# Out-degrees as rows of sums: a count matrix streamed past a column of ones in a two-layer graph network

## The reference

```python
h = maximum(layernorm(x), 0)
# layer 0: row = src, col = dst
h0 = h @ W_in + b_in                                   # 3125 x 64
deg = segment_sum(ones(50000), row, 3125)              # how many edges start at each node
dis = where(deg > 0, rsqrt(maximum(deg, 1)), 0)
cur = acc = h0
for _ in range(3):
    cur = segment_sum(cur[col] * (dis[row] * dis[col])[:, None], row, 3125)
    acc = acc + cur
x = x + (acc / 4) @ W_out + b_out
# layer 1: relational, 64 edge types built of 16 bases
h = maximum(layernorm(x), 0)
x = x + relu(segment_sum(msg(h[src], type, weight), dst, 3125) + h_bias + h @ loop_weight)
```

## Time and profile before

| | us |
|---|---|
| median of 3 runs | 986.79 (985.37 to 989.05) |
| profiled execution: time | 984.78 |
| profiled execution: span of the trace | 983.2 |
| PE busy / PEld busy | 785.8 / 584.1 |
| DVE busy | 719.5 |
| ACT busy / POOL busy | 355.4 / 471.9 |
| the 625 one-column products, first to last start | 239.8 to 297.3 |

### The profile page before, as it was taken

One profiled execution on the slowest core, in us unless ns is written; L12 is line 12 of the kernel. 1 busy time (PEld: TensorE's weight loads), 2 busy tenths in 40 slices (PEclk: granted clock), 3 DMA queues, 4 the chain that ended last, 5 costly groups with the idle time before them and its releaser, 6 DMA issues.

```text
span 983.2 us, 27231 instructions
## 1 busy us (share of the span) xinstructions
PE 785.8 (80%) x5974; PEld 584.1 (59%) x5975; DVE 719.5 (73%) x2379; ACT 355.4 (36%) x705; POOL 471.9 (48%) x568
## 2 busy tenths in 40 slices
PE   5666666667879999999179899898888888787876
PEld 3234333333558999998057677676666666555555
DVE  7999999998625644435167777777777877887885
ACT  0422577898760000013154444433433332222100
POOL 2186433231000000101377777777777777777773
PEclk8798999999658999999579999999999999999999
DMA  4022457896330000112951221221211111211213
GB/s 123 22 67 67 117 138 141 159 170 144 98 94 6 2 2 1 34 41 87 293 139 51 54 53 51 53 54 51 53 53 52 53 52 52 54 51 53 54 51 93
DMA packets 64853, 73.32 MB, mean 75 GB/s; under 512 B 12804, under 2 KB 53179, under 8 KB 64667
## 3 DMA queue, kind: packets, MB, share of 16 engines
q1 hardware_dynamic: 48362, 37.30, 15.3%
q0 software_dynamic: 16432, 35.29, 14.3%
HBM read 43.85 MB, written 8.22 MB: 53 GB/s over the span
## 4 chain that ended last, share of the span: by engine, by line
PE 34%; DVE 26%; issue 15%; DVEq 10%; POOL 8%; DMA 5%; ACT 2%; SPq 1%; POOLq 0%; ACTq 0%
PE ps L1211 16%; PE ps L1288 10%; POOL CT L677 7%; DVE ohbuf L843 7%; DVE CT L985 5%; DVE u L843 4%; DMA CT<-h_dram,src_col 4%; PE ps L1119 4%; DVE CT L988 3%; DVEq L988 3%; DVEq L127 3%; PE ps L1267 2%; DVEq L985 2%; DVE ohbuf L838 2%; DVEq L843 1%
## 5 line engine op out<-in xcount | busy, mean ns | idle before, releaser
L677 POOL DMA_INDIRECT CT<-h_dram,src_col x391 | 370.5, 948 | 126.7 <-issue 105.4
L1288 PE MATMUL ps<-CT 128*128 128x256 f32 x1180 | 302.6, 405 | 65.4 <-DVE CT L985 31.7
L1288 PEld LDWEIGHTS ps<-CT 128*128 128x128 f32 x1180 | 203.0, 191 | 159.2 <-issue 142.1
L988 DVE SCALAR_TENSOR_TENSOR CT<-ps,dlP,CT 128x256 f32<-128x256 f32 x580 | 279.4, 482 | 4.5
L985 DVE COPY CT<-CT 128x128 f32 x590 | 148.3, 251 | 123.6 <-PE ps L1288 54.7
L1430 ACT COPY CT<-ps 128x256 f32<-128x256 f32 x200 | 77.6, 388 | 307.1 <-PE ps L1288 303.6
L1119 PE MATMUL ps<-ohbuf 128*128 128x400 bf16 x395 | 103.5, 368 | 42.3 <-DVE ohbuf L843 18.6
L1368 ACT CAST stage<-ps 128x800 bf16<-128x800 f32 x100 | 82.3, 823 | 75.6 <-PE ps L1119 74.5
L1211 PE MATMUL ps<-u,CT 128*128 128x192 bf16 x1250 | 105.0, 246 | 0.9 <-DVEq L951 0.9
L1211 PEld LDWEIGHTS ps<-u,CT 128*128 128x128 bf16 x1250 | 103.1, 98 | 1.9 <-DVEq L951 1.1
L843 DVE TENSOR_SCALAR ohbuf<-iota,keys 128x400 bf16<-128x400 int16 x395 | 103.1, 324 | 0.0
(11 more groups left out here) (186 smaller groups left out, 619.5 us busy)
## 6 DMA issues: line engine op xcount, KB each, us to landing
CT<-stage SPq DMA_DIRECT2D x200, 100.0 KB, 3.5
u<-types_dram POOLq DMA_DIRECT2D x49, 128.0 KB, 3.6
CT<-h_dram,src_col POOLq DMA_INDIRECT x391, 2.5
coef_dram<-coef_out POOLq DMA_DIRECT2D x49, 64.0 KB, 3.8
CT<-coef_dram SPq DMA_DIRECT2D x1, 3048.0 KB, 11.0
out<-CT SPq DMA_DIRECT2D x4, 256.0 KB
ohbuf<-x SPq DMA_DIRECT2D x3, 320.0 KB, 3.8
x_dram<-ohbuf SPq DMA_DIRECT2D x3, 320.0 KB, 2.7
```

The lines of the kernel that those rows point to most:

```text
L677: pool.indirect_dma_start(out=gring[:, (j + 1) % GRING, :], out_offset=None, in_=h2_dram, in_offset=bass.IndirectOffsetOnAxis(ap=src_col[: ...
L988: dve.scalar_tensor_tensor(kpair[:, u, :, :], nodes.unsqueeze(1).broadcast_to([P, BASES, WIN]), dl, coef_flat[:, ds(tiles * -BASES + NT * ...
L1288: pe.matmul(ps[:, ds(summed.place(counts[u][0], RING), 1), 0:WIN * BASES], gpair[:, u, :], kpair[:, u, :, :].rearrange("p b d -> p (b d)") ...
```

## The change

The degree sums are turned round. The stationary operand becomes a matrix of seven columns, all zero but one column of ones (a slice of `pick_row`, chosen so that the ones stand at column `i`), and `CT[:, k, :]` is streamed past it, 512 columns at a time: seven products for a group `k` (six of 512 columns and one of 128) instead of 25. Row `i` of bank 7 collects the sums of sources 512 i to 512 i + 511. At the end ACT copies the 7 x 512 sums to SBUF (`deg_rows`, in the space of `keys`), and four float32 products with an identity turn them to columns in the bank `COEF_BANK`, in another order of columns, which DVE's two comparisons read in two pieces each. POOL makes `pick_row` at the start (two memsets and a wait), so that the count on which DVE and PE wait at the start, `PC0`, is 14 instead of 12. The twelve products of zeros stand behind the turning and go to bank 7.

```diff
+SPANS = -(-NPAD // 512)
-PC0 = 12
+PC0 = 14
+        pick_row = sb("pick_row", [P, 2 * SPANS], BF16)
+        deg_rows = keys[0:SPANS, 0:512]
@@ gpsimd, at the start
+            pool.memset(pick_row[:], 0.0).then_inc(pool_c, 1)
+            pool.wait_ge(pool_c, 11)
+            pool.memset(pick_row[:, SPANS - 1:SPANS], 1.0).then_inc(pool_c, 1)
             pool.memset(ones_bf[:], 1.0).then_inc(pool_c, 1)
@@ vector
             dve.wait_ge(deg_done, 1)
-            deg = ps[:, 7, 0:NG]
-            step(dve.tensor_scalar(small[:, 2, :], deg, 1.0, None, ALU.max))
-            dve.sem_inc(deg_cut, 1)
-            step(dve.tensor_scalar(small[:, 3, :], deg, 0.0, None, ALU.is_gt), False)
+            whole = NG // 4
+            for at, op in ((2, ALU.max), (3, ALU.is_gt)):
+                sums = ps[:, COEF_BANK, 0:4 * SPANS].rearrange("p (j i) -> p i j", j=4)
+                bound = 1.0 if op == ALU.max else 0.0
+                step(dve.tensor_scalar(small[:, at, 0:4 * whole].rearrange("p (i j) -> p i j", j=4), sums[:, 0:whole], bound,
+                                       None, op), False)
+                step(dve.tensor_scalar(small[:, at, 4 * whole:NG], sums[:, whole, 0:NG - 4 * whole], bound, None, op))
+                if op == ALU.max:
+                    dve.sem_inc(deg_cut, 1)
@@ tensor, add_degrees(k)
-                for m in range(NG):
-                    last = pe.matmul(ps[:, 7, m:m + 1], CT[:, k, m * P:(m + 1) * P], ones_bf[:, 0:1],
-                                     start=False, stop=True, skip_group_check=True)
+                for i in range(SPANS):
+                    n = min(512, NPAD - i * 512)
+                    last = pe.matmul(ps[0:SPANS, 7, 0:n], pick_row[:, SPANS - 1 - i:2 * SPANS - 1 - i],
+                                     CT[:, k, i * 512:i * 512 + n], start=False, stop=True, skip_group_check=True)
@@ tensor, behind the last group
+            last.then_inc(deg_summed, 1)
+            pe.wait_ge(coef_cp, CT_TURNS)
+            pe.wait_ge(deg_copied, 1)
+            for j in range(4):
+                last = pe.matmul(ps[:, COEF_BANK, j * SPANS:(j + 1) * SPANS], deg_rows[:, j * P:(j + 1) * P],
+                                 ident[0:SPANS, 0:SPANS], start=True, stop=True)
             last.then_inc(deg_done, 1)
-            pe.wait_ge(coef_cp, CT_TURNS)
             for _ in range(IDLE_MM):
-                pe.matmul(ps[:, COEF_BANK, :], zb, zw, start=True, stop=True)
+                pe.matmul(ps[:, 7, :], zb, zw, start=True, stop=True)
@@ scalar, behind the last windows
+            act.wait_ge(deg_summed, 1)
+            act.copy(deg_rows, ps[0:SPANS, 7, 0:512]).then_inc(deg_copied, 1)
             act.wait_ge(deg_cut, 1)
```

More of the change, by code:

```diff
@@ L367, in build @@
         passed = sem("passed")
+        deg_summed = sem("deg_summed")
+        deg_copied = sem("deg_copied")
         deg_done = sem("deg_done")
```

## The result

| | before | after |
|---|---|---|
| median | 987.10 us (14 runs) | 989.62 us (14 runs) |
| lowest to highest | 984.41 to 991.31 | 988.92 to 992.49 |
| profiled execution: time / span | 984.78 / 983.2 | 988.92 / 987.3 |

The account below looks back on a forecast made before the run. PE, partly at half clock, was taken to bound the degree stretch (239 to 298 us). Turns -0.9, last groups +1.4, turning +1.0 and start +0.3 gave +1.8 us, from 986.8 to 988.6; range 984 to 995.5.

Parts of the forecast that it names:

- blocks, nine times: Turns 49 to 57, block start to next half A: 2.67 us instead of 1.93, nine times 0.74, +6.7 us.
- pair phases at the full clock, sequencer ahead: Nine pair phases between blocks: five turns without a wait -5.1 us, four with one -2.5 us.
- last seven groups: From turn 58's block to the last group's end: 9.5 us instead of 8.07, transfer wait gone, +1.4 us.
- turning, less the zeros that ended late: Ahead of layer 0: copy, turning products, handovers and comparison 1.8 us, less 0.77 for zeros no longer last, +1.0 us.
- start and before the first block: Kernel start: POOL's two memsets and a wait delay DVE, +0.3 us, or 0 if the edge loads cover it.
- The clock: PE's clock at the full level for the whole stretch, 1.0 from 239 to 298 us, where it was 0.67 and 0.50.
- Both rivals on the clock: Clock falls in turn 58: +12.5 us, 999, chance 0.10; half clock throughout: +44, 1031, chance 0.04.
- The hole: PE's 0.41 us idle at each turn's register load vanishes behind a wide block; if kept, blocks cost +10.4 instead of +6.7.
- the rival of a faster stream: Wide products quicker than one column a 2.4 GHz cycle: -6.3 us, 980.5; chance 0.05, shared with turns gaining more.
- The pairs: Half A and B pairs, turns 49 to 57: five turns without a wait fall 15.1 to 10 us, four with one 17.1 to 14.6.
- The case that ACT holds half B back in all turns: Rival: shorter pairs make half B wait in the five plain turns, losing half of 5.1 us: +4.4, 991.2; no separate chance.
- Nothing runs ahead on PE: Rival: the 0.41 us hole stays (+3.7), pairs stay at 2.37 a turn (+1.9): +7.4 us, 994; chance 0.19.

Follow-up runs that it names:

- early groups in the one-column form: Kernel before with degree groups spread over turns 41 to 57 as one-column products, two zeros products behind each block from turn 49: 984.65 us, ratio 0.9974.
- the zeros behind and ahead of the block: Two runs: kernel before plus two 512-column zeros products in turns 49 to 58, behind the one-column block (984.43 us, 0.9975) or ahead of it (992.29 us, 1.0061).
- The kernel with the lowest median here: Changed kernel with early groups, 19 instead of 22 done by turn 57, so five fill the wait behind turn 58: 983.21 us, ratio 0.996.
- the run with early groups: Changed kernel with one group behind each of turns 41 to 48 and 22 done by turn 57: 988.01 us, ratio 1.0005.

## Why the prediction was right

| step | forecast us | in the two traces us |
|---|---|---|
| blocks, nine times | +6.7 | 25.2 against 17.5: +7.7 |
| pair phases at the full clock, sequencer ahead | -7.6 | 24.2 against 32.1: -7.9 |
| last seven groups | +1.4 | 9.62 against 8.07: +1.5 |
| turning, less the zeros that ended late | +1.0 | 5.77 against 4.49 from sum to layer 0: +1.3 |
| start and before the first block | +0.3 | 240.31 against 239.79: +0.5 |
| layer 0 starts | +1.8 | +3.15 |
| time | +1.8 | +2.5 (1.5 to 3.6) |

The mechanism came out term by term; that the median moved by nearly what was forecast is in part luck. Layer 0 starts 3.15 us later, where the terms gave 1.8, and the two profiled executions are 4.1 us apart (988.92 and 984.78): that of the kernel before lies 2.3 us below its median, that of the change 0.7.

**The clock** was forecast at the full level for the whole stretch, from the 0.99 of the sparse stretch ahead of it; it is 1.00 from 239 to 323. Both rivals on the clock are out. The 0.99 was a mean: between 217 and 225 us the clock was 0.79 in the kernel before, with no degree product in sight. That the clock shortened the pairs is shown from the other side: with the clock restored in part by zeros, the one-column kernel gains 3.6 of 7.9 us there. But it is not all of it. With one-column products and zeros at a clock of 1.00 (early groups in the one-column form) the pair phases are 27.0 us, and in a turn without a wait ten pairs take 2.33 to 2.39 us, as the 2.37 of turn 53 in the earlier trace rows, where behind a wide block they take 1.80. So about 5 of the 7.9 us are the clock's and some 2.8 come with the wide block itself; the prediction had put them down to a sequencer that is ahead, which fits, though no run isolates it.

**The hole** at the register load was forecast to vanish behind a wide block; it has (240.31 to 243.10). The 0.16 of the earlier trace rows against the 0.84 of the earlier trace rows was the right pair of rows, and the zeros behind and ahead of the block show the rule by itself: 0.7 us for 3.9 us of products behind, all of it and the hole besides ahead. The reading that a hole shrinks by about the length of the queued work does not hold for one-column products: 25 of them (0.63 us) leave 0.42 to 0.48 us, fifty (1.25 us) leave 0.39 to 0.43, where nothing else ended later.

**The block** was mis-sized, 2.67 instead of 2.79, nine times 0.12. Of that, 14 x 0.0025 us are what a product takes beyond its columns at the full clock; I had left it out although layer 0's 82.5 ns for 80 ns of columns shows it. The other 0.09 lies between the last product, which streams 128 columns in 0.05 us and starts at 242.95, and the first pair at 243.10; that it is the pair's weight load, 0.10 us, which does not fit under so short a product, is argued and not shown. The Trainium skill, page "TensorE: Matmul & The Clock Gate", section "Back-to-back issue gap", has N / 2.4 + 2.5 ns for a product by itself, with which the 49 products in 9.62 us agree (by it an estimate of 9.46, with 0.16 of modelled end behind the last); its sustained 131 ns for 512 columns does not hold here, and with it falls the rival of a faster stream.

**The pairs**: the four turns with a wait inside were forecast at 14.6 us and the five others at 10; they took 14.6 and 9.6. The times from half A to half B were forecast at 2.4, 2.5, 2.35 and 2.9 and came at 2.43, 2.43, 2.35 and 2.77. The prediction put the wait down to ACT in all four; in the kernel before the profile names DVE in turns 50 and 57, and ACT in all four only after the change. The case that ACT holds half B back in all turns came once, in turn 53 (half B of 259.97, 0.25 us of waiting); the rest had slack, as its 77% said. **Nothing runs ahead on PE** is out with the hole.

**The last groups and the turning** are the two costs that the change brings and that no clock pays back. They were sized to 0.1 and 0.3 us, and the run without the turning gives its 1.8 to 2.1 us by subtraction. The missing 0.3 are the 0.16 us by which DVE's chain grew (3.68 to 3.84 from its first comparison to L927's end) and 0.11 from DVE's signal to PE, which before was covered by the zeros.

What is left of the 3.15 us at layer 0 against 1.8 forecast: 1.0 blocks, -0.3 pairs, 0.1 last groups, 0.3 turning, 0.2 ahead of the first block: DVE's later start is 0.2 of those 0.5 us, and the rest lies in turns that are the same in both kernels.

## What to carry to other kernels

Where an engine's clock is throttled, count what a change does to the clock and to the work apart: here 7.9 us won in the pairs, 5 of them by the clock, and 7.7 us of extra columns were nearly equal, and two products of zeros, put where the sequencer would have left a hole, bought nearly half of the first for a tenth of the second. Look at what the engine does in the last wait of a stage: waits of 4.0 and 4.35 us put the work behind them at the half clock, while the waits of up to 1.75 us inside the change's turns did not. The kernel with the lowest median here is the one that moved useful products into that wait, as many as fit and no more.

## What the runs showed of the hardware that was not expected

- The same two 512-column products a turn hold the clock behind a block of one-column products (0.89 over 44 us in one execution) and not ahead of it (0.66). The medians are 7.9 us apart; by the traces a third of the difference is the pairs at the lower clock, the rest the zeros' own time.
- Ten pairs at the full clock take 2.33 to 2.39 us behind one-column products and zeros, and 1.80 behind fourteen wide products.
- Eight groups of wide products in turns 41 to 48, where DVE sets the pace, took 11.6 us of PE and moved turn 49's block by +0.9 us in one run and -0.1 in another. With them the clock was 1.00 from 208 to 239 us, where both kernels without them have 0.94.
- A register load on PE's sequencer leaves 0.84 us behind pairs, 0.4 behind fifty one-column products (at either clock), 0.42 to 0.48 behind 25, and nothing behind work that is queued for longer than the load.
- 4 us of idle PE ahead of a stage cost 2.3 us in the stage's first 250 products (23.12 against 20.80 us); in the run with early groups 4.35 us of idle time cost 2.5 us up to layer 0 (9.8 us from the last group's start, against 7.3).
